# A two-layer graph network on one core: tiles paired in another order, bases split every second slot

## What is computed

```
h   = relu(layernorm(x))                                   # x: 1250 nodes x 512
out = segment_sum(h[src] @ weight[etype] * edge_weight, dst)   # 40000 edges
      # weight[r] = sum_b w_comp[r, b] * bases[b]; 32 relations, 8 bases, 512 x 512
x   = x + out + h_bias
h   = relu(layernorm(x)) @ W.T + b
dis = rsqrt(1 + out_degree);  loops are added to the edges
x   = x + relu(segment_sum(dis[row] * dis[col] * h[row], col))
```

## Time and profile before

| | us |
|---|---|
| median of 3 runs | 617.85 |
| lowest, highest | 615.9, 618.54 |
| the profiled execution | 612.81 |
| its span, from the first instruction to the last | 611.0 |
| TensorE, DVE, POOL, ACT busy in the span | 491.6, 347.5, 358.1, 152.3 |

### The profile page before, as it was taken

One profiled execution on the slowest core, in us unless ns is written; L12 is line 12 of the kernel. 1 busy time (PEld: TensorE's weight loads), 2 busy tenths in 40 slices (PEclk: granted clock), 3 DMA queues, 4 the chain that ended last, 5 costly groups with the idle time before them and its releaser, 6 DMA issues.

```text
span 611.0 us, 16039 instructions
## 1 busy us (share of the span) xinstructions
PE 491.6 (80%) x5902; PEld 313.8 (51%) x5902; DVE 347.5 (57%) x971; ACT 152.3 (25%) x272; POOL 358.1 (59%) x473
## 2 busy tenths in 40 slices
PE   3031446397999999999999999998999999989984
PEld 1021435265666666665565556555555565555531
DVE  7798137976575435755554754788646543332045
ACT  3392224552232011222220220320313202123010
POOL 3333626876676776775765757768747777760000
PEclk9655655699999999999999999998999999999986
DMA  8896965557786887795884867856867877773106
GB/s 281 295 351 225 392 187 145 160 160 201 221 273 202 243 271 225 215 277 176 251 254 144 273 208 221 273 179 189 268 178 212 255 238 237 239 231 107 33 11 162
DMA packets 53109, 132.32 MB, mean 217 GB/s; under 512 B 12109, under 2 KB 18110, under 8 KB 53030
## 3 DMA queue, kind: packets, MB, share of 16 engines
q0 software_dynamic: 27040, 99.60, 53.7%
q1 hardware_dynamic: 25036, 30.47, 16.0%
q10 hardware_dynamic: 954, 1.13, 0.6%
HBM read 120.32 MB, written 10.84 MB: 215 GB/s over the span
## 4 chain that ended last, share of the span: by engine, by line
PE 53%; DVE 13%; DMA 12%; issue 8%; ACT 5%; POOL 4%; SPq 3%; ACTq 1%; DVEq 0%
PE PS L1636 24%; PE PS L1614 17%; DMA gath<-rows_layer,srcs 7%; PE PS L1643 5%; PE PS L1684 4%; POOL gath L766 4%; DMA types<-types_by_slot 2%; SPq L624 2%; DVE room_b L1278 2%; ACT room_b L885 2%; DVE zt L1278 1%; DMA edge_records<-room_c 1%; DMA w1t<-edge_records,w1t 1%; DVE room_b L1347 1%; PE PS L1620 1%
## 5 line engine op out<-in xcount | busy, mean ns | idle before, releaser
L766 POOL DMA_INDIRECT gath<-rows_layer,srcs x335 | 341.8, 1020 | 168.8 <-issue 86.7
L1614 PE MATMUL PS<-sel,gath 128*128 128x48 f16 (+7 forms) x4020 | 315.7, 206 | 40.4 <-DVE zt L1278 12.1
L1614 PEld LDWEIGHTS PS<-sel,gath 128*128 128x128 f16 x4020 | 245.5, 102 | 164.6 <-issue 71.7
L1636 PE MATMUL PS<-room_b,zt 128*128 128x512 f16 x480 | 163.8, 385 | 1.4 <-DVE sel L1200 1.4
L1636 PE MATMUL PS<-room_b 128*128 128x512 f16 (+1 forms) x480 | 151.1, 380 | 0.9 <-DMA gath<-rows_layer,srcs 0.4
L1620 PE MATMUL PS<-oh_ad,gath 128*128 128x30 bf16 (+7 forms) x335 | 64.7, 193 | 0.0
L1194 DVE TENSOR_TENSOR masks<-iota_n,dloc 128x24 bf16<-128x24 f32 (+12 forms) x92 | 17.9, 195 | 80.9 <-issue 44.5
L1643 PE MATMUL PS<-u_t,room_c 128*128 128x512 f16 (+2 forms) x180 | 57.5, 404 | 3.7 <-issue 2.1
L1636 PEld LDWEIGHTS PS<-room_b 128*128 128x128 f16 (+1 forms) x480 | 47.3, 104 | 14.8 <-DVE room_b L1278 0.6
L826 ACT CAST val<-val_f 128x64 f16<-128x64 f32 x42 | 11.0, 261 | 168.4 <-DVE val_f L1151 163.4
L1636 PEld LDWEIGHTS PS<-room_b,zt 128*128 128x128 f16 x480 | 45.1, 99 | 5.9 <-issue 1.5
(11 more groups left out here) (227 smaller groups left out, 436.4 us busy)
## 6 DMA issues: line engine op xcount, KB each, us to landing
room_b<-in_L_gnn_bases_dram SPq DMA_DIRECT2D x8, 1024.0 KB, 9.9
gath<-rows_layer,srcs POOLq DMA_INDIRECT x335
types<-types_by_slot SPq DMA_DIRECT2D x168, 16.0 KB
x_t<-x_base SPq DMA_DIRECT2D x19, 128.0 KB, 5.0
u_t<-in_x_dram SPq DMA_DIRECT2D x9, 256.0 KB, 6.2
x_base<-u_t SPq DMA_DIRECT2D x9, 256.0 KB
x_layer<-x_t SPq DMA_DIRECT2D x16, 128.0 KB, 4.1
gath<-x_layer SPq DMA_DIRECT2D x16, 128.0 KB, 2.8
```

Source lines behind the costliest of these rows:

```text
L766: pool.indirect_dma_start(out=gath[:, s % UN, :], out_offset=None, in_=tab0_d[:, :], in_offset=bass.IndirectOffsetOnAxis(ap=srcs[:, s:s + ...
L1614: mm(there, gath[:, s % UN, D * t + P * f:D * t + P * (f + 1)], sel_parts[:, here, k, 0:NB * w, u], start=first and t == 0 and u == 1, sto ...
L1636: last = mm(PS[0:r, PBANK[q], :], zt[q % 2][:, t, f, b, 0:r], base_hl[:, b, u, f, :], start=(m == 0), stop=(m == NM - 1))
```

## The change

Four things change together.

1. **Pairs.** Before, pair p held the tiles 2p and 19-2p: a long tile with a short one, and the order of pairs began with the middle (25 slots in the first pair, 78 in the last). Now pair p holds 2p and 2((8-p) mod 10)+1, so that tiles 18 and 19 make one pair and the others turn by one place; the pairs run in rising order of length, 14 slots in the first, 82 in the last.
2. **Bases** are split every second slot, at slots 10, 12, ... 24.
3. **The planner** may start products at slot 24 in place of 26. Its rules are the same, but due slots follow the tiles: it now deals out three products in a slot where it dealt two until slot 66.
4. **Set-up.** The table of row factors has four kinds of blocks in place of two, in four transfers in place of three (DVE line 982 runs 8 times in place of 4), and DVE has two more linked operations on 336 columns ahead of the first selections, one more ahead of the last tiles' degrees.

```diff
-    PORDER = [5, 4, 6, 9, 3, 7, 2, 8, 1, 0]
-    PAIR = [(2 * p, NTI - 1 - 2 * p) for p in range(NT)]
-    PAIR_OF = [t // 2 if t % 2 == 0 else (NTI - 1 - t) // 2 for t in range(NTI)]
+    PORDER = [9, 3, 4, 5, 6, 2, 7, 1, 8, 0]
+    TURN = NT - 2
+    PAIR_OF = [t // 2 if t % 2 == 0 else (TURN - t // 2) % NT for t in range(NTI)]
+    PAIR = [(2 * p, 2 * ((TURN - p) % NT) + 1) for p in range(NT)]
...
+    SIDES = [tuple(PAIR_OF[2 * k + h] >= HA for h in range(2)) for k in range(NT)]
+    KINDS = sorted(set(SIDES))
...
-        H_AT = S0[RH] - 12
+        H_AT = S0[RH] - 2
...
         for n in range(NB):
-            STEPS[BS_AT + 3 * n].append(("bsplit", n))
+            STEPS[BS_AT + 2 * n].append(("bsplit", n))
...
-            GATHER, LAND, FREE, READY, RESERVE, FIRST = 5.8, 12.0, 14.0, 15.0, 14, 26
+            GATHER, LAND, FREE, READY, RESERVE, FIRST = 5.8, 12.0, 14.0, 15.0, 14, 24
...
-            for s in range(2):
+            for s, kind in enumerate(KINDS):
                 for h in range(2):
...
+            link(v.tensor_scalar(code_f, tile_f, -MID - 0.5, float(HA), ALU.is_lt, ALU.mult))
+            link(v.tensor_tensor(tile_f, tile_f, code_f, ALU.add))
```

More of the change, by code:

```diff
@@ L36, in gnn_kernel @@
     NTI = 2 * NT
-    PORDER = [5, 4, 6, 9, 3, 7, 2, 8, 1, 0]
-    PAIR = [(2 * p, NTI - 1 - 2 * p) for p in range(NT)]
-    PAIR_OF = [t // 2 if t % 2 == 0 else (NTI - 1 - t) // 2 for t in range(NTI)]
+    PORDER = [9, 3, 4, 5, 6, 2, 7, 1, 8, 0]
+    TURN = NT - 2
+    PAIR_OF = [t // 2 if t % 2 == 0 else (TURN - t // 2) % NT for t in range(NTI)]
+    PAIR = [(2 * p, 2 * ((TURN - p) % NT) + 1) for p in range(NT)]
+    assert all(PAIR_OF[t] == p for p in range(NT) for t in PAIR[p])
+    SIDES = [tuple(PAIR_OF[2 * k + h] >= HA for h in range(2)) for k in range(NT)]
+    KINDS = sorted(set(SIDES))
+    RUNS = [(k, next((m for m in range(k, NT) if SIDES[m] != SIDES[k]), NT)) for k in range(NT) if not k or SIDES[k] != SIDES[k - 1]]
+    RUNS = [(lo, hi) for lo, hi in RUNS if hi < NT] + ([(RUNS[-1][0], NT - 1)] if RUNS[-1][0] < NT - 1 else []) + [(NT - 1, NT)]
+    NTAB = NT + len(RUNS)
+    MID, WHOLE = (TURN % HA) / 2, TURN / 2
     TORDER = [t for p in PORDER for t in sorted(PAIR[p])]
@@ L229, in gnn_kernel @@
         gap_max = take_g(f32, SL)[0:1, :]
-        assert all(TROWS[i] == TN for i in TORDER[:-1])
         rec = rec_w[0:EP, :].rearrange("p (c k) -> p c k", k=4)
@@ L603, in load_base @@
                 sp.dma_start(base_in[:, n + 2, :, :], bases[n, :, :].rearrange("(f p) o -> p f o", p=P)).then_inc(s_bin[n], 16)
[L605 to L609 removed]
+            sp.wait_ge(s_ident_fac, 2 * len(KINDS))
+            for lo, hi in RUNS:
+                kind = KINDS.index(SIDES[lo])
+                if hi < NT:
+                    sp.dma_start(tab0_d[P * lo:P * hi, 2 * D:ROW].rearrange("(t p) c -> p t c", p=P).bitcast(bf16),
+                                 ident_fac[:, kind, :].unsqueeze(1).to_broadcast([P, hi - lo, P])).then_inc(s_tab0, 16)
+                else:
+                    sp.dma_start(tab0_d[P * lo:N, 2 * D:ROW].bitcast(bf16), ident_fac[0:XROWS[lo], kind, :]).then_inc(s_tab0, 16)
             for i in range(NT):
@@ L731, in _ @@
             for r in range(NTI):
-                last = g.memset(gap_max[:, LAST[r]:LAST[r] + 1], float(WIN[r] - TN if r + 1 < NTI else TN - TROWS[TORDER[r]]))
+                last = g.memset(gap_max[:, LAST[r]:LAST[r] + 1], float((WIN[r] if r + 1 < NTI else TN) - TROWS[TORDER[r]]))
             last.then_inc(s_gap, 1)
@@ L1168, in _ @@
             values_full(1)
-            link(v.scalar_tensor_tensor(tile_f, tile_f, -float(HA // 2), code_f, ALU.add, ALU.add))
+            link(v.scalar_tensor_tensor(tile_f, tile_f, -MID, code_f, ALU.add, ALU.add))
             one_hot_types(2)
@@ L1175, in _ @@
             values_low(1)
-            link(v.scalar_tensor_tensor(tile_f, tile_f, float(HA // 2), win_c, ALU.add, ALU.mult))
+            link(v.scalar_tensor_tensor(tile_f, tile_f, MID, win_c, ALU.add, ALU.mult))
             link(v.tensor_tensor(code_f, tile_f, dloc_f, ALU.add))
@@ L1215, in _ @@
                     v.tensor_scalar(any_own[:, h:h + 1], part_f[:, :], 1.0 - TN * h, None, ALU.add)
-                dve.wait_ge(s_tab0, 16 * (NT + 3))
+                dve.wait_ge(s_tab0, 16 * NTAB)
                 dve.wait_ge(s_val, VEARLY)
```

18 lines of the change are left out of this document (7 added, 11 removed).

## The result

| | before | after |
|---|---|---|
| median, us | 616.88 | 632.03 |
| lowest, highest | 614.38, 618.54 | 630.75, 633.66 |
| span of the profiled execution | 611.0 | 629.0 |

The ratio is 1.0272 (95% interval 1.0235 to 1.0309). The forecast was 632.4. The medians differ by 15.2 and 17.9 us, the two profiled spans by 18.0; the forecast's sum was 14.6.

The account below looks back on a forecast made before the run. It took TensorE to wait for DVE in the start, fill the middle, and follow the gathers' pace in the tail. Terms summed to +14.6 us on the median 617.85, giving 632.4; range 617 to 642.

Parts of the forecast that it names:

- The third flush: Start of the kernel: DVE begins this flush near 131.9 us, slot 29 ends near 135.3; start loses 3.9 us.
- half clock: TensorE stops some 5 us ahead of the third flush, then runs at half speed: 2.5 us added (0 to 3.4).
- Projection 2: Behind slot 118 and a lookup, it waits for DVE's flush and reading: 3.8 us (1.0 to 5.5).
- The middle: Tile 0 begins four slots earlier but with 17 more products and one more degree step done: +1.7 us.
- the stop that was to go: The stop at slot 238 and the half speed behind it partly vanish: -1.8 us (-3.6 to 0).
- The tail: From slot 253 to slot 334, at the gathers' pace, 100.9 us: +4.2 us (2.5 to 5.5).
- Set-up: Extra row-factor operations, a transfer and linked operations, mostly hidden by DVE's wait for types: +0.3 us (0 to 1.5).
- Gathers beside splits: Splits lengthen gathers at 97 to 130 us, but TensorE waits for DVE's flush then: 0, up to 1 us.
- The middle catches up: Rival: with three products per slot, TensorE's waits for gathers could go; 620.9 us, or 614.3; chance 0.19.
- The clock stays low: Rival: half speed lasts longer after both new stops, costing about 6.8 + 1.7 us; 638.4 us; chance 0.12.
- The gathers are not hidden: Rival: the ring runs dry at the third flush and 9.7 us come on top; 642.1 us; chance 0.06.

Follow-up runs that it names:

- e_double: Changed kernel with VectorE making the low half of the last base twice; 634.74 us, 1.0365 of the kernel before.
- e_bs2: Kernel before with only its base splits moved to every second slot instead of every third; 620.38 us, 1.0064 of the kernel before.
- e_hist: Changed kernel with the steps for the last pair's degrees moved later; 631.65 us, 1.0281 of the kernel before.
- e_both: Changed kernel with the last pair's degree steps later and projection 2 two slots later; 624.85 us, 1.0169 of the kernel before.
- e_rise3: Changed kernel's program with the old pairs in rising order of length and splits every third slot; 623.37 us, 1.0129 of the kernel before.
- e_turnb3: Changed kernel with the 14-slot pair seventh, splits every third slot, products from slot 26; 626.14 us, 1.0225 of the kernel before.
- e_after: Changed kernel run again without an edit, beside the kernel before; 632.20 us, 1.0285 of the kernel before.

## Why the prediction came out, step by step

**The third flush, right.** Predicted at 131.9, between 127 and 134.6; it started at 132.16. DVE's waits for ACT were taken as 5 us and came to 6.0 in four places. Slot 29 was put at 135.3 and ended at 137.27, because this slot, matched bank by bank to the flush, itself ran at clock 0.50 until about 136.7, where slot 38 before did not. So the term "half clock" lies ahead of the slot's end: start, half clock and set-up were counted as 3.9 + 2.5 + 0.3 = 6.7 and measured 5.85. That DVE's work sets this start is shown by e_double; e_bs2 shows that in the old order the spacing of the change lengthens it.

**Projection 2, right in place and kind, too small.** The stop was predicted at 4.2 us (4.5 less the lookup's 0.3), of which 0.4 was taken as there anyway, and measured 4.38. The failing step is the decision to leave the half clock out of the likeliest value and to put it into the high bound at 1.7: the whole projection ran at half speed, 2.55 us more. The term is 6.8 between e_hist and e_both, where 3.8 was counted and 5.5 allowed. The row that was used for the bound, the stop at slot 238, had narrow slots waiting for gathers behind it; here 2.6 us of dense matmuls stood there.

**The middle, and the stop that was to go.** +1.7 and -1.8 were counted. Without projection 2's 6.8, 0.4 of the 7.2 us from slot 29 to slot 253 are left, for -0.1 predicted. But the reason given for the -1.8 is wrong: tile 1's narrow slots have their stop too (1.79 us, with clock 0.58 over the window from 416 to 420 above), and when e_hist took its cause away, the gathers made another of 2.13. The waits for gathers grew, too: between slot 29 and slot 253 TensorE waited 9.4 us for them in 14 places, before between slot 38 and slot 257 7.8 in 11. So something else in the middle gave back about as much; which, no run tells. That these two terms agree with the sum is partly luck, and e_rise3 and e_turnb3 say so: other orders of the same work lost some 6 and 7 us in the middle, where far less was expected of them.

**The tail, right, but for one stop.** 100.9 us predicted from slot 253 to slot 334, 101.9 measured, +4.9 for +4.2; e_turnb3 has 101.1 with the same last pair. The second profile of the changed kernel (e_after) has 103.4, +6.4, which is over the high bound of 5.5. Both have a stop that the prediction didn't price and the kernel before doesn't have: at slot 265 a turn waits 2.1 us for DVE to read a lookup, again two steps that meet; in the second profile half clock came behind it (last section).

**Set-up.** +0.87 in the landing of the types for +0.3, inside its bounds. It is of the size of the spread: the profiles of other kernels with the new set-up have the landing at 84.66 to 85.88, those with the old one at 83.80 to 84.76.

**Gathers beside splits, right.** The 15 gathers that began between 96.9 and 131 us took 24.3 us, 10.0 more than at 0.95 each. (The prediction's 28.67 us before end at the window's edge; those 20 gathers took 29.96, 11.0 more.) In this stretch TensorE waited for DVE and for no gather, so 0 was right. With the Trainium skill's exclusive lock (SBUF — State Buffer, SBUF: two separate sides) the trace agrees more closely than the prediction read it. Before and after, 14 of the 15 gathers that began while a split ran ended 0.82 to 0.87 us behind the split's end, as the second of these two does behind the split of 128.85 to 131.20; the first, which ran already when that split began, took its 0.95:

```profile
128.49 0.95 POOL L776 DMA_INDIRECT gath<-rows_layer,srcs  x1 [0.30 <-issue]
129.74 2.29 POOL L776 DMA_INDIRECT gath<-rows_layer,srcs  x1 [0.30 <-issue]
```

The eight splits are 18.8 us and the gathers grew by about half of that, since a split holds up only the gather that comes behind its start.

**The rivals.** *The middle catches up* falls: TensorE waited 14.7 us in 25 places for gathers, where 2 was the mark. *The clock stays low* falls: the clock was back at 1.00 by 136.7, 3.6 us after TensorE had started again at 133.08, where the rival's measure was 13.7; at projection 2 the half clock cost 2.55 us for the rival's 1.7. *The gathers are not hidden* falls: what ended TensorE's stop of 5.59 us there was DVE's flush, not a gather.

**The total.** The profile's terms add up to 18.0, the forecast to 14.6; 3.0 of the difference is projection 2. The median after, 632.03, met the forecast because the two medians of the first comparison lie 15.2 us apart, and because it was counted from 617.85, 1.0 above the median before of that comparison; the second pair lies 17.9 apart. The sum was 2 to 3 us too small, and the agreement to 0.4 us is chance.

## What to carry to other kernels

Where two engines run through a hand-written order, look first for places where steps meet that wait for each other: here one projection behind a lookup and a flush cost 1.1 per cent, more than any other single piece that a run took out. Price such a stop with the half clock behind it, by what stands right behind: dense matmuls pay in full. Where work of two engines has to be done before some late point, like the splits, look at what one waits for of the other, and not only at how much work there is: splits every third slot, every second, and in two rows behind flushes made 1.000, 1.006 and 0.993 of the same kernel, with the same busy time of DVE ahead of the third flush.
